# Count work of a two-network graph kernel regrouped into bursts of slots, with GpSimd waiting for TensorE at their ends

## The reference

```python
def _gine_layer(x, src, dst, edge_attr, W1l, b1l, gl, bl, W2l, b2l):
    msg = jax.nn.relu(x[src] + edge_attr)
    agg = jax.ops.segment_sum(msg, dst, num_segments=N_NODES)
    h = (x + agg) @ W1l + b1l
    ...                      # batch norm, relu
    h = jax.nn.relu(h @ W2l + b2l)
    return jax.nn.relu(h)
def _gin_conv(x, edge_index, wA, bA, wB, bB, eps):
    src, dst = (edge_index[0], edge_index[1])
    agg = jax.ops.segment_sum(x[src], dst, num_segments=x.shape[0])
    h = (1.0 + eps) * x + agg
    h = jax.nn.relu(h @ wA.T + bA) @ wB.T + bB
    return h
```

## Time and profile before

| | us |
|---|---|
| median of 3 runs | 2762.56 (2761.05 to 2769.45) |
| span of the profiled execution | 3625.8 |
| edges of layer 0, gathers from 72.9 | to 1261.3 |
| edges of layer 1, gathers from 1329.4 | to 2580.3 |
| layer 2, gathers from 2670.6 | to 3091.2 |
| layer 3, gathers from 3154.9 | to 3568.1 |

### The profile page before, as it was taken

The page is one execution under the profiler, slowest core; times in us unless marked ns, Lnnn a source line. Parts: engine busy times, 40 slices in busy tenths (PEclk is TensorE's granted clock), DMA queues, the critical chain, the costliest instruction groups (busy, mean ns, idle before and its releaser), DMA issues.

```text
span 3625.8 us, 35066 instructions
## 1 busy us (share of the span) xinstructions
PE 2077.8 (57%) x9399; PEld 1269.9 (35%) x9399; DVE 1694.3 (47%) x2880; ACT 734.2 (20%) x1002; POOL 1941.4 (54%) x2048
## 2 busy tenths in 40 slices
PE   2454545545555552454545554535568778778888
PEld 1332323323332332232323232323334444444445
DVE  5655556555555553465646564545652122312112
ACT  3121212212122241222222222223340000300001
POOL 5655656555655526565655565556234555265552
PEclk7676667766767776777777777776778888888889
DMA  5232322323233332333333333334324444344442
GB/s 153 79 98 82 94 90 91 97 83 102 89 102 93 101 98 67 105 102 106 104 103 112 111 110 112 114 107 131 107 90 160 131 156 139 95 153 158 135 133 83
DMA packets 228544, 396.82 MB, mean 109 GB/s; under 512 B 43080, under 2 KB 133020, under 8 KB 228388
## 3 DMA queue, kind: packets, MB, share of 16 engines
q0 software_dynamic: 65024, 133.30, 14.3%
q1 hardware_dynamic: 111684, 162.15, 12.8%
q10 hardware_dynamic: 51680, 99.63, 7.8%
HBM read 333.10 MB, written 61.81 MB: 109 GB/s over the span
## 4 chain that ended last, share of the span: by engine, by line
another core or an unknown queue 29%; PE 24%; issue 21%; DVE 12%; ACT 9%; DVEq 3%; ACTq 2%; POOL 0%; DMA 0%; SPq 0%
PE psA L1536 13%; PE psG L1551 5%; ACT xp_room L785 3%; ACT psG L758 3%; DVE cell_room L1116 3%; DVE xp_room L1130 2%; DVEq L1051 2%; DVE hid L1076 2%; PE psA L1493 1%; PE psG L1509 1%; DVE xp_room L1095 1%; ACT count_out L741 1%; ACTq L751 1%; PE psG L1600 1%
## 5 line engine op out<-in xcount | busy, mean ns | idle before, releaser
L674 POOL DMA_INDIRECT xg<-node_table,src_all x1520 | 1438.1, 946 | 1087.4 <-DVE xp_room L1130 566.7
L1493 PE MATMUL psA<-cell_room,xp_room 128*128 128x512 f16 (+1 forms) x2336 | 712.5, 450 | 967.5 <-ACT count_out L741 609.5
L694 POOL DMA_INDIRECT xg<-node_table,idx x480 | 467.9, 975 | 519.9 <-issue 358.4
L1493 PEld LDWEIGHTS psA<-cell_room,xp_room 128*128 128x128 f16 x2336 | 258.7, 114 | 1384.3 <-ACT count_out L741 658.2
L1130 DVE TENSOR_TENSOR xp_room<-psG,xg 128x512 f32<-128x512 f32 x380 | 255.3, 672 | 938.8 <-ACT psG L758 910.9
L1116 DVE TENSOR_SCALAR cell_room<-psG,cell_all 128x932 f16<-128x932 int16 x1088 | 683.8, 683 | 16.7 <-remote 16.7
L1509 PE MATMUL psG<-hid,xp_room 128*128 128x160 f32 x3072 | 522.2, 336 | 265.3 <-DVE hid L1076 208.2
L1509 PEld LDWEIGHTS psG<-hid,xp_room 128*128 128x128 f32 x3072 | 504.4, 221 | 304.5 <-issue 302.0
L758 ACT COPY psG<-xp_room 128x512 f32<-128x512 f32 x384 | 226.7, 590 | 1486.0 <-issue 692.8
L1029 DVE TENSOR_TENSOR acc<-acc,row_slot 128x38 f32 x192 | 38.3, 200 | 636.9 <-ACT row_slot L837 529.3
L1536 PE MATMUL psA<-cell_room,xp_room 128*128 128x456 f16 x1200 | 274.8, 383 | 98.1 <-issue 76.1
(11 more groups left out here) (156 smaller groups left out, 817.4 us busy)
## 6 DMA issues: line engine op xcount, KB each, us to landing
xp_room<-in_edge_attr_dram ACTq DMA_DIRECT2D x95, 768.0 KB
cell_room<-count_store SPq DMA_DIRECT2D x16, 2850.0 KB
count_store<-count_out SPq DMA_DIRECT2D x96, 465.5 KB
hid<-count_store SPq DMA_DIRECT2D x16, 2736.0 KB
xg<-node_table,src_all POOLq DMA_INDIRECT x1520
xp_room<-in_edge_attr_dram ACTq DMA_DIRECT2D x95, 256.0 KB
row_slot<-node_table SPq DMA_DIRECT2D x1024, 0.5 KB
hid<-node_table SPq DMA_DIRECT2D x1024, 0.5 KB
```

Source lines behind the costliest of these rows:

```text
L674: nc.gpsimd.indirect_dma_start(xg[:, n % 2, u, j, :], None, x if n < RAW_TURNS else table, bass.IndirectOffsetOnAxis(ap=src_all[:, s, j:j ...
L694: nc.gpsimd.indirect_dma_start(xg[:, q, u, j, :], None, table, bass.IndirectOffsetOnAxis(ap=idx[:, q, u, j:j + 1], axis=0),).then_inc(row_ ...
L1493: last = nc.tensor.matmul(psA[:, bank, 0:w], src_hot[:, hots(n) % 2, at, :], cells[:, c % CELL_RING, c0:c0 + w], start=first, stop=end)
```

## The change

The planner at the head of the file sets, for each unit k, a gate slot `UNIT_GATE[k]`: the slot after the one with its last chunk, at least two slots behind the gate before. Longer stretches are split by further gates into bursts of at most 6 slots. There are 109 gates, 39 in layer 0 and 70 in layer 1.
- POOL, before the first gather of the slot behind a gate, waits until TensorE has used the last piece of the unit (at a gate without a unit: the last piece that stands before it).
- ACT evicts a unit at its gate, no longer in the slot of its last chunk.
- TensorE takes the pieces of the next unit in the step behind the gate, which can lie in the next turn.
- `load_behind` is gone from ACT. SP issues the same two loads (`load_ahead`), ahead of its row fetches of the turn and waiting for the product of turn n - 2; its stores of units stand behind the row fetches.
- `cells` has 12 buffers, the further 6 in `rows_h`; `src_hot` has 3. DVE waits for the stored table of the layer before it uses `rows_h`.

```diff
+def unit_gates():
+    gates, last = [], -1
+    for k in range(UNITS):
+        built = SLOT_OF[(UNIT_END[k] - 1) // 2]
+        stop = (built // SLOTS // TURNS + 1) * TURNS * SLOTS - SLOTS - 1
+        last = min(max(built + 1, last + 2), stop)
+        gates.append(last)
+    return gates
...
+def piece_step(c, p0):
+    k = UNIT_OF[2 * c + p0 // HALF]
+    return max(SLOT_OF[c], UNIT_GATE[k - 1] + 1) if k > 0 else SLOT_OF[c]
...
+def burst_gates():
+    gates = {g: UNIT_USED[k] for k, g in enumerate(UNIT_GATE)}
+    for layer in range(2):
+        bounds = [(layer * TURNS + RAW_TURNS) * SLOTS - 1] + [g for g in UNIT_GATE if g // SLOTS // TURNS == layer]
+        for a, b in zip(bounds, bounds[1:]):
+            parts = -(-(b - a) // LONGEST_BURST)
+            for i in range(1, parts):
+                g = a + (b - a) * i // parts
+                gates[g] = max(USED_AFTER[c] for c in range(CHUNKS) if piece_step(c, PIECES[c][-1][0]) < g)
+    return gates
...
+            def load_ahead(n):
+                if not RING <= n < EDGE_TURNS:
+                    return
+                used = n - RING
+                sp.wait_ge(scattered[used % 2], sp.snap(rounds * (used // 2 + 1) + 1))
+                load_turn(n)
...
-                    for k in units_in(turn_chunks(n)):
-                        sp.wait_ge(count_evicted, k + 1)
-                        sp.dma_start(count_store[k], count_out[:, k % 2, :]).then_inc(count_stored[k % 2], 16)
+                    load_ahead(n + 1)
                     gather_rows(layer, n % TURNS)
+                    for u in range(SLOTS):
+                        for k in units_at(n * SLOTS + u):
+                            sp.wait_ge(count_evicted, k + 1)
+                            sp.dma_start(count_store[k], count_out[:, k % 2, :]).then_inc(count_stored[k % 2], 16)
...
                     for u in range(SLOTS):
+                        if n * SLOTS + u - 1 in BURST_GATE:
+                            pool.wait_ge(cells_used, BURST_GATE[n * SLOTS + u - 1])
...
-                            if u == (SLOTS - 1 if n == RAW_TURNS else 1):
-                                load_behind(n - 1)
-                            units_out(slot_chunks(n, u))
+                            units_out(i)
...
-                slot = hots(n) % 2
-                if n >= 2 and turn_chunks(n - 2):
-                    dve.wait_ge(cells_used, USED_AFTER[turn_chunks(n - 2)[-1]])
...
+                slot = hots(n) % HOT_RING
+                if n % TURNS == RAW_TURNS:
+                    dve.wait_ge(table_written, 16 * LG * (n // TURNS + 1))
+                if hots(n) > HOT_RING:
+                    dve.wait_ge(cells_used, USED_AFTER[turn_chunks(COUNTING[hots(n) - 1 - HOT_RING])[-1]])
```

More of the change, by code:

```diff
@@ L92 @@
 RING = 3
-CELL_RING = 6
+CELL_RING = 12
+ROOM_CELLS = 6
+HOT_RING = 3
+LONGEST_BURST = 6
 EDGE_TURNS = 2 * TURNS
@@ L187 @@
 LAYERS = 4
-assert TURNS % 2 == 1 and 2 * SLOTS * EPP * WIN <= CELL_RING * CB
+assert TURNS % 2 == 1 and 2 * SLOTS * EPP * WIN <= ROOM_CELLS * CB
 assert SUPERS % SLOTS == 0 and OVERLAP % EPP == 0 and SECOND <= P
@@ L192 @@
 assert CB % 2 == 0 and CB - IOTA <= IOTA <= 1024 and MOST_CHUNKS <= CELL_RING and EPP * D == 512
-assert CBANKS == 4 and UPG * CW <= 512 and HALF_B * UPG >= CELL_RING * BLOCKS // 2
+assert CBANKS == 4 and UPG * CW <= 512 and HALF_B * UPG >= ROOM_CELLS * BLOCKS // 2
 def group_blocks(g):
@@ L733, in centre_raw, with units_out @@
                     last.then_inc(raw_centred, 1)
-            def units_out(chunks):
-                for k in units_in(chunks):
+            def units_out(i):
+                for k in units_at(i):
                     act.wait_ge(cells_used, UNIT_USED[k])
@@ L742, in units_out @@
                              ).then_inc(count_evicted, 1)
[L744 to L751, removed]
             def stage_attributes(i):
@@ L1474, in turn_rows, with build_counts @@
                     last.then_inc(cols_turned, 1)
-            def build_counts(n):
-                chunks = turn_chunks(n)
-                for i, c in enumerate(chunks):
-                    if i == 0:
-                        pe.wait_ge(src_hot_ready, hots(n))
-                    for p0, p1 in PIECES[c]:
-                        k = UNIT_OF[2 * c + p0 // HALF]
-                        first = 2 * c + p0 // HALF == UNIT_END[k] - UNIT_SIZES[k]
-                        end = 2 * c + p1 // HALF == UNIT_END[k]
-                        if first and k > 0:
-                            pe.wait_ge(count_evicted, k)
-                        pe.wait_ge(cells_ready, 2 * (c + 1))
-                        at = len(chunks) + parted(chunks).index(c) if p0 else i
-                        for bank in range(CBANKS):
-                            c0 = bank * 512
-                            w = min(512, CB - c0)
-                            last = nc.tensor.matmul(psA[:, bank, 0:w], src_hot[:, hots(n) % 2, at, :],
-                                                    cells[:, c % CELL_RING, c0:c0 + w], start=first, stop=end)
-                        last.then_inc(cells_used, 1)
+            def build_counts(i):
+                for c, p0, p1 in STEPS.get(i, ()):
+                    n = TURN_OF[c]
+                    chunks = turn_chunks(n)
+                    if c == chunks[0] and p0 == 0:
+                        pe.wait_ge(src_hot_ready, hots(n))
+                    k = UNIT_OF[2 * c + p0 // HALF]
+                    first = 2 * c + p0 // HALF == UNIT_END[k] - UNIT_SIZES[k]
+                    end = 2 * c + p1 // HALF == UNIT_END[k]
+                    if first and k > 0:
+                        pe.wait_ge(count_evicted, k)
+                    pe.wait_ge(cells_ready, 2 * (c + 1))
+                    at = len(chunks) + parted(chunks).index(c) if p0 else c - chunks[0]
+                    for bank in range(CBANKS):
+                        c0 = bank * 512
+                        w = min(512, CB - c0)
+                        last = nc.tensor.matmul(psA[:, bank, 0:w], src_hot[:, hots(n) % HOT_RING, at, :],
+                                                cells[c % CELL_RING][:, c0:c0 + w], start=first, stop=end)
+                    last.then_inc(cells_used, 1)
             def edge_windows(layer, n):
@@ L1521, in edges @@
                         pe.wait_ge(flag_ready, 2)
-                    build_counts(n)
+                    for u in range(SLOTS):
+                        build_counts(n * SLOTS + u)
                     edge_windows(layer, n)
```

33 lines of the change are left out of this document (22 added, 11 removed).

## The result

The change makes the kernel slower, by 8.25%: 2990.03 us (median; 2984.24 to 2997.66) against 2761.81 (2760.59 to 2769.45) measured beside it, ratio 1.0825, 95% interval 1.0807 to 1.0843, 228 us. The forecast was 2888.

What follows compares the result with a forecast made beforehand. GpSimd's gathers, at 1.2 to 1.25 us each, were taken as the bound, with hardly a pause. Gate waits of 125 us added to 2762.6 gave 2888 us, all other parts nothing; range 2730 to 3000.

Steps and rivals of the forecast that it cites:

- The profile's extra 863 us: First profile of the kernel before: pauses of some 5.6 us a turn read as cost of recording, absent from timed runs.
- Gates behind slot 1: Eight GpSimd gates asking for m = 3 or 4 pieces: 6.7 and 7.5 us each, together 55 us.
- free gates: 33 gates (30 behind slot 0, 3 behind slot 1) needing only pieces of the turn before: nothing.
- the last: Gate in turn 96, asking for the last unit, whose pieces follow the product of turn 96: 17 us, once.
- The count of pieces m: TensorE has used m pieces of turn n at 7.3 + 0.8m us after turn n - 1's hot rows end.
- the product's 6.5 us: TensorE's product of turn n - 1, ahead of the pieces, taken as 6.5 us because gates leave TensorE idle before it.
- Gates behind slots 2 and 3: 33 gates behind slot 2, 0.1 to 4.1 us each, 50 us; 35 behind slot 3, 3 us, besides the last's 17.
- the sum follows the start of the slot's last gather by 2.6 us: DVE's sum starts 2.6 us after GpSimd's last gather of the slot starts; used to place GpSimd at every gate.
- ScalarE's two issues: ScalarE loses two load issues, 0.4 and 0.5 us a turn, and the wait for the product: nothing in timed runs.
- the extra cells, the third hot slot: 12 cell buffers and 3 hot slots leave the same DVE instructions: nothing.
- The half-clock rival: TensorE's clock stays at half, each gate with m pieces 0.5 + 1.0m dearer: 3000 to 3110 us; with late SyncE 0.09.
- No change: Rival: GpSimd reaches gates later or sums have slack for waits of 1 to 3 us: 2755 to 2771 us, chance 0.09.

Runs made afterwards that it cites:

- the loads moved: Kernel before with only the two attribute loads a turn issued by SyncE in place of ScalarE: 2760.95 us, ratio 0.9995.
- small loads: Changed kernel with SyncE's two attribute loads a turn cut from 128 to 16 partitions from turn 3 on: 2945.31 us, ratio 1.0661.
- The square: Four kernels with gates: pieces in old place, ScalarE loads 2842.0 us, SyncE loads 2861.7; pieces held (as in the change), 2970.3 and 2990.0.
- the old order: Kernel before with only the 109 gates added; pieces, evictions and loads as before: 2841.96 us, ratio 1.0289.

## Why the prediction was right, and where it was not

- **What bounds.** Right. GpSimd's gathers at 1.25 us hold the time of the kernel before: fewer gathers give 1.19 us each, the loads moved give nothing. The working had no clean profile and got this from a count against the timed median. It took 290 us of gaps from the first profile; in the second they are 195 (13.6, 44.2, 65.1, 38.6, 33.4), and the same division, (2762.6 - 195) / 2032, gives 1.26 us beside the 1.25 that it settled on.
- **The profile's extra 863 us.** Right that timed runs do not have them. I called them the cost of recording as if every profile of this kernel paid it, and forecast 3400 to 3700 for the changed one. It was 2982. That step was wrong: one odd profile does not tell of the next.
- **Gates behind slot 1, free gates, the last.** 55, 0 and 17 us forecast, 56.0, 2.1 and 17.1 found. The count of pieces m and the product's 6.5 us (5.98 to 7.55 at the gates that waited) were good, a piece 0.8.
- **Gates behind slots 2 and 3.** The step that failed is "the sum follows the start of the slot's last gather by 2.6 us". It does where nothing is in the way; behind a unit's store and the attribute loads it was up to 7.55 at the gates that waited. I had asked whether SyncE's loads come in time for their own user, and priced them at nothing, and not what they do to the rows that travel beside them. At full size the two classes cost 119.5 us, with small loads 77.9, against 53 forecast.
- **The pattern behind slot 2.** I had said that the waits would be long with m of 4 to 6 and short elsewhere. They are not: the 21 gates with m of 1 to 3 cost 63.6 us in place of 13, the 12 with 4 to 6 cost 27.1 in place of 36. With small loads the forecast's order comes out, 0.3, 2.2, 2.8, 2.8, 3.2 and 4.4 us a gate for m of 1 to 6, where the working has 0.1, 0.9, 1.7, 2.5, 3.3 and 4.1. So the count of pieces was sound, and the late rows hid it. Why the gates with m of 4 and 5 cost less with the full loads than with small ones (2.0 against 3.0 us) is open.
- **Row turns.** In turns 26 and 75 slot 2 is fetched by SyncE, so GpSimd comes to the gate 5 us early. The working put it where a full turn would have it. Turn 26's gate cost 8.6 us in place of 0.9, turn 75's 7.9 in place of nothing (8.1 and 4.3 with small loads, so late rows have a part of the second).
- **Turn 2.** The count took every turn as a steady one. At the start TensorE is far behind: 33.3 us at the first gate in the trace, 7 to 12 of them gone when that gate is taken out.
- **The two layers.** Layer 1 was to grow by three times what layer 0 does. It grew by 152 us and layer 0 by 70 (edges from turn 2 on), of which turn 2's gate has 33.
- **The held pieces.** They were in the count through m, but not priced by themselves. The square does: with the gates there, 128 us of the 228, more than the gates cost in the old order (80); without gates, 9 us at most. For the gates in the old order I had expected 2890 or more, by the same mechanism (pieces behind the product of the turn before); it does not hold there, so that working was right for the new order alone.
- **ScalarE's two issues, the extra cells, the third hot slot.** Priced at nothing; the rest of the change costs 9 us, all told.
- **Clock.** The granted clock of layer 1 fell from 0.81 in the kernel before to 0.76 (window by window, below), between the levels of 1.2 and 2.4 GHz as forecast. The half-clock rival did not come. A product took 6.79 us in the median of layer 1 against 6.37, and TensorE's busy time is the same (below), so the fall is a small part of the loss at most. The Trainium skill (TensorE: Matmul & The Clock Gate, section Why this matters for your kernels) asks for matmuls without idle gaps between bursts; the trace agrees in direction: TensorE idles 8.8 us ahead of a product in the median of layer 1, 3.8 before, the clock fell, and it did not gain from grouping the pieces.

The windows of the two kernels over layer 1, changed kernel first, the kernel before by its second profile (window, us, busy of PE, PEld, DVE, ACT, POOL, granted clock, DMA share, GB/s):

```profile
1109.00:2229.00 1120.00, 587.31 (x2748) 427.14 (x2748) 681.87 (x1076) 324.20 (x361) 732.95 (x775) 0.76 0.41 121
```

```profile
1041.00:2009.00 968.00, 585.88 (x2741) 410.20 (x2742) 680.17 (x1076) 323.72 (x361) 731.72 (x776) 0.81 0.45 139
```

Every engine does the same work in both; only the stretch is 152 us longer.

- **Range and rivals.** 2990 lies in the range, 10 us below its upper end. The size of the loss was short by 103 us, with the mechanism right. Of these the size of the loads has 42, turn 2's gate 33 and the two row turns some 11; the 17 left have no run of their own. That the median lies inside owes more to the width of the range than to the sum: three terms held, and the two that failed most (late rows, turn 2) were priced at nothing. "No change" would have needed slack between GpSimd and the gates; only the free gates and part of those behind slot 3 have it.

What stays open: how the 128 us of the held pieces divide between the order of the pieces, the late evictions, the place of the stores and the added buffers, which were not taken apart, and whether gates a turn later would be free.

## What to carry to other kernels

When one engine paces a stage by issuing work back to back, a wait on another engine in its queue costs close to the full time by which that engine is behind, at each place; work that is moved behind a long product should be priced at the gate that asks for it. A large transfer can cost nothing for its own user and still delay a small one that travels beside it: ask which waits end on a DMA before moving it. And if a profile's span is far from the timed median, take another profile before reading its waits.

## What the runs showed of the hardware

- One profile of a kernel was 31% longer than its timed runs (3625.8 against 2762.56 us), with SyncE's register moves at up to 1406 ns; a second of the same kernel was not (2760.5, 29 ns), nor was that of any of the twelve other kernels.
- The user of rows gathered by an indirect DMA began 2.6 us after the gather's start with nothing in the way, 4.4 with a 465.5 KB store and 0.13 MB of loads issued beside it, and 7.55 with the store and 1 MB of loads.
- SyncE issued 48 row fetches in 18.2 to 18.7 us, but took 21.9 us a turn with its register loads and stores.
